# Conv attention: query projection around the output product, shared normalisation; second attention: small products in 128x32 tiles

## The chip, the cores and the metric

The kernel runs on one core of a Trainium2 chip. The metric is the device time of one execution in microseconds (us). The core has TensorE (products, and loads of the stationary operand), VectorE, ScalarE, GpSimd and SyncE (here a queue of DMA issues). Each works through its own instructions in order and waits on semaphores for the others.

## What is computed

Four images of 256 channels x 32 x 32 (1024 tokens of 256) go through three blocks. Cut to what matters:

```python
# block 1, attention by 1x1 convolutions, IC = 128
k, v, q = conv(x, wk, bk), conv(x, wv, bv), conv(x, wq, bq)           # (b, IC, n)
attn = softmax(einsum('bcn,bcm->bnm', v, q), axis=2)
o = bn2(conv(bn1(conv(einsum('bcn,bnm->bcm', k, attn), wwg)), wout))
x = relu(o + x)
# block 2, on tokens: 8 heads of 32
t = tokens(x)
q, k, v = split(layernorm(t) @ w_qkv)
t = t + softmax(q @ k.T * 256 ** -0.5) @ v @ w_out + b_out
# block 3: layer norm, router (top 2 of 8 experts), expert MLPs 256 -> 1024 -> 256 with gelu
t = t + moe(layernorm(t))
```

## The kernel before

One program is written out by hand for each engine; semaphores, each with a name, tie them together. Three phases follow each other.

**Conv phase**, `tokens(b)` for the images b = 0 to 3, in each engine's block. TensorE makes eight score blocks (`scores`), ScalarE their exponentials, TensorE weighs the keys with them (`weigh`, bank PP[3]). VectorE scales the result to `y1` in two halves. TensorE multiplies `woT` with `y1` (the output product, semaphore `cv_made`), VectorE adds the image (`cv_kept`), ScalarE applies Relu (`x1_kept`). TensorE turns the result into tokens in three groups (`turned_tokens`, line 1153: group 0 in PP[1], 1 in PP[3], 2 in PP[2]); ScalarE copies each group (lines 863 and 864, `tk_kept_a`, in the order 1, 0, 2; a copy of group 0 or 2 waits for VectorE's statistics of that group, `bst_kept`). ScalarE takes the root of the variances, VectorE normalises eight blocks of tokens to `ln` (line 1690), TensorE turns `ln` into `lnT` (line 1172, banks PP[0] and PP[1]), and ScalarE and VectorE copy it as high and low halves. Then come the query, key and value products of block 2.

Between these, for the next image b + 1, TensorE makes the first projections of block 1: `project_q` in two halves over the input channels (PP[0]), `project_v` (PP[1], which waits for the second token copy, `tk_kept_a`), `project_k` (PP[2], which waits for the third). ScalarE keeps the high halves (`keep_q`, `keep_v`), VectorE the low ones (`q_low_half`, `v_low_half`), and `keep_k`. ScalarE and GpSimd also split the expert weights into high and low halves in this phase (`split_weights(b, i)`, eight per image, with loads queued on GpSimd).

**Second attention**, `attend(b)`, 32 steps per image. A step makes four chunks of scores (`score_chunk`, line 1334, four 32-column tiles with 97 rows), the row maxima of a later group (`max_group`, line 1253, 32-row tiles; two VectorE reductions, line 1740, must leave its banks first), the weighing and the sums of an earlier step (`weigh_heads`, line 1306, and `sum_heads`, lines 1316 and 1321: 128 rows, four 32-column tiles). ScalarE makes the exponentials, GpSimd adds pairs of them. In every fourth step `max_row` turns the eight maxima of 128 queries into a row (line 1262). For b >= 1 the steps 2, 3, 4, 6, 7, 8, 10 and 11 also project 128 tokens of the image before (`tail_project`, whose products are recorded at line 1022, 128x264); VectorE adds them to the residual. The last image's eight projections stand in the last four steps, after the last two weighings, and the last two in the first expert tile.

**Experts**, 40 tiles of tokens in f16 products at full width, and the output.

Of the kernel before, what the change touches and what calls it, by code (L numbers as in the profile page):

```python
# [8 lines left out]
ALU = mybir.AluOpType  # L9
# [3 lines left out]
P = 128  # L13
B, C, N = 4, 256, 1024
CC = C // P
# [25 lines left out]


LOAD_GROUP = 16 * 7
LOAD_MAX = 16 * 2
# [70 lines left out]
def hybrid_block(nc, x, wk, bk, wv, bv, wq, bq, wwg, bn1_g, bn1_b, bn1_m, bn1_v, wout, bout,  # L115
# [20 lines left out]
    with ctx:  # L136
# [185 lines left out]
        def ring(last):  # L322
            return 2 if last else 3

        def qk_bank(u, last):
            return PP[(2, 3, 2, 0)[u]] if last else PP[(u + 2) % 4]
# [33 lines left out]
        for name in ("ld_qv ld_vec ld_first wqv_kept q_low v_low ld_w ld_x0 ld_x1 ld_y0 ld_y1 bst_kept ld_we we_kept mh_made pool_const pe_prep dve_prep act_prep "  # L360
                     "q_made v_made k_made q_kept v_kept k_kept sc_made max_kept exp_kept ks_kept "
                     "av_made y1_kept cv_made cv_kept x1_kept tk_made tk_kept_a stat_kept "
                     "sd_kept ln_kept lnT_made lnT_kept_a lnT_kept_v qk_made qhi_kept qlo_kept vt_made "
                     "vt_kept_a vt_kept_v res0_kept st_res0 st_v st_q0 st_q1 "
# [447 lines left out]
        def _(act):  # L812
# [29 lines left out]
            def tokens(b, last):  # L842
# [9 lines left out]
                for c in range(CC):  # L852
                    act.wait_ge(s("cv_kept"), b * 2 + (c + 1))
                    act.activation(XB[b][:, c], XB[b][:, c], ACT.Relu, bias=vec[:, BE2 + c:BE2 + c + 1])\
                       .then_inc(s("x1_kept"), 1)
                act.wait_ge(s("st_v"), FREE + b * 16)
                for g in (1, 0, 2):
# [10 lines left out]
                if not last:  # L868
                    keep_q(b + 1)
                    keep_v(b + 1)  # L870
                if last:
                    act.wait_ge(s("wT_made"), 1)
                    act.activation(woTf, PP[3][:, 0:HALF].rearrange("p (c i n) -> p c i n", c=CC, i=CC), ACT.Copy)\
                       .then_inc(s("wT_kept"), 1)
                else:
                    split_weights(b, 5)
                for c in range(CC):
                    act.wait_ge(s("lnT_made"), b * 2 + (c + 1))
                    act.activation(lnT[:, c, 0], PP[c][:, :], ACT.Copy).then_inc(s("lnT_kept_a"), 1)
                if last:  # L880
                    act.wait_ge(s("wp_made"), 1)
                    act.activation(wp_early[:, :, :], PP[3][:, HALF:HALF + CC * E].rearrange("p (c e) -> p c e", c=CC),
                                   ACT.Copy).then_inc(s("we_kept"), 1)
                    split_weights(b, 5)
                for u in range(4):
                    act.wait_ge(s("qk_made"), b * 4 + (u + 1))
                    if u >= 2:
                        act.wait_ge(s(f"st_q{u % 2}"), FREE + b * 64 + 32)
                    act.activation(qs[:, u % 2, 0], qk_bank(u, last)[:, :], ACT.Copy,
                                   scale=(C ** -0.5 if u < 2 else 1.0) / WSCALE).then_inc(s("qhi_kept"), 1)  # L890
                    if u < 2:
                        split_weights(b, 6 + u)
                act.wait_ge(s("vt_made"), b * 2 + 1)
                act.wait_ge(s("st_res0"), FREE + b * 16 + 16)
# [123 lines left out]
        def _(pe):  # L1018
# [22 lines left out]
            def project_q(n, c):  # L1041
                if c == 0 or not n:
                    pe.wait_ge(s(f"ld_{'xy'[n % 2]}{c}"), n // 2 * 16 + 16)
                if n and not c:
                    pe.wait_ge(s("cv_kept"), 2 * n - 1)
                    pe.wait_ge(s(f"ld_{'xy'[n % 2]}1"), n // 2 * 16 + 16)
                mm = project_half(n, PP[0], wqT, c)
                if c == CC - 1:
                    mm.then_inc(s("q_made"), 1)
# [47 lines left out]
            def tokens(b, last):  # L1097
# [35 lines left out]
                for i in range(NT):  # L1133
                    if i + ring(last) < NT:
                        scores(i + ring(last))
                    if last:
                        early_max(i)
                    weigh(i)
                for c in range(CC):
                    for h in range(2):  # L1140
                        pe.wait_ge(s("y1_kept"), b * 2 + (h + 1))
                        product(PP[c][:, h * HALF:(h + 1) * HALF], [(woT[:, c], y1[:, h * HALF:(h + 1) * HALF])],
                                "cv_made" if h else None)
                if not last:
                    project_q(b + 1, 0)
                for c in range(CC):
# [10 lines left out]
                if not last:  # L1157
                    project_q(b + 1, 1)
                    project_v(b + 1)
                    project_k(b + 1)  # L1160
                    pe.wait_ge(s("q_low"), b + 2)
                    pe.wait_ge(s("v_low"), b + 2)
                else:
# [4 lines left out]
                    router_turned()  # L1168
                for c in range(CC):
                    for t in range(NT):  # L1170
                        pe.wait_ge(s("ln_kept"), b * NT + (t + 1)) if c == 0 else None
                        mm = pe.transpose(PP[c][:, t * P:(t + 1) * P], ln[:, t, c * P:(c + 1) * P], identf[:, :])
                    mm.then_inc(s("lnT_made"), 1)
# [84 lines left out]
            def max_row(b, u, before):  # L1258

                bank = next_slot(b, before)  # L1260
                pe.wait_ge(s("nm_kept"), b * UNITS + (u + 1))
                pe.transpose(bank[0:2 * GH, 0:P], mx[:, :], identf[:, :]).then_inc(s("c_made"), 1)


            def tail_project(t, b, before, n):
# [5 lines left out]
                if n == 1 and t == 0:  # L1271
                    pe.wait_ge(s("ld_wo"), 16)
                    pe.wait_ge(s("wp_kept"), 1)
                tok_at = slice(t * P, (t + 1) * P)
                product(bank[:, 0:WIDE], [(OS[:, k, tok_at], wo_sb[:, k]) for k in range(CC)], "c_made")

# [237 lines left out]
        def _(dve):  # L1514
# [106 lines left out]
            def tokens(b, last):  # L1621
# [37 lines left out]
                for c in range(CC):  # L1659
                    dve.wait_ge(s("cv_made"), b * 2 + (c + 1))  # L1660
                    dve.scalar_tensor_tensor(out=XB[b][:, c], in0=PP[c][:, :], scalar=vec[:, S2 + c:S2 + c + 1],
                                             in1=XB[b][:, c], op0=ALU.mult, op1=ALU.add).then_inc(s("cv_kept"), 1)
                for g in (0, 2, 1):
                    made, of = turned_tokens(g)
# [22 lines left out]
                if b == 0:  # L1687
                    dve.wait_ge(s("st_zero"), 32)
                for t in range(NT):
                    dve.tensor_scalar(ln[:, t], tok[:, t], mv[:, t, 0:1], small[:, 3, t:t + 1],  # L1690
                                      ALU.subtract, ALU.mult).then_inc(s("ln_kept"), 1)
                dve.tensor_tensor(lgp[:, 0], lgp[:, 0], lgp[:, 1], ALU.add)
                dve.drain()
                dve.tensor_tensor(lg0[:, b], lgp[:, 0], per_expert(lb0[:, :], NT), ALU.add)
                if not last:
                    q_low_half(b + 1)
                    v_low_half(b + 1)
                    keep_k(b + 1)
                for c in range(CC):
                    dve.wait_ge(s("lnT_kept_a"), b * 2 + (c + 1))  # L1700
                    dve.tensor_tensor(lnT[:, c, 1], PP[c][:, :], lnT[:, c, 0], ALU.subtract)\
                       .then_inc(s("lnT_kept_v"), 1)
                dve.wait_ge(s("ln_kept"), b * NT + NT)
                dve.tensor_tensor(tok, tok, bob.unsqueeze(1).broadcast_to((P, NT, C)), ALU.add)\
# [597 lines left out]
```

## Time and profile before

| | |
|---|---|
| median of three runs | 1163.66 us (1159.1 to 1166.8) |
| the profiled execution | 1163.12 us, of which its span 1161.3 |
| TensorE busy | 1087.0 us, 94% of the span |
| VectorE, ScalarE, GpSimd busy | 816.4, 629.6, 594.3 us |
| conv phase | to about 289 us |
| second attention | about 289 to 726 us |

In the profile PE is TensorE's products, PEld its loads of weights, DVE VectorE, ACT ScalarE, POOL GpSimd, SP SyncE; L1022 is line 1022 of the kernel. One f32 product of 512 columns stands there as two records. A chain of waits is followed back from the last instruction: at each step to what released it.

### The profile page before, as it was taken

How to read it: one execution, taken by the hardware profiler on the slowest of the kernel's cores; microseconds unless marked ns; L12 is line 12 of the kernel's file. 1: busy time of each engine (PE TensorE's matmuls, PEld its weight loads, DVE VectorE, ACT ScalarE, POOL GpSimd, SP SyncE). 2: the span in 40 equal slices, each digit the busy share in tenths (PEclk: the TensorE clock that was granted, in tenths of full speed). 3: DMA queues.
4: the chain of work that ended last, by engine and by line, in shares of the span. 5: the costliest groups of instructions: out<-in, count | busy, mean ns of one | idle time of the engine just before them, and what ended most of it. 6: DMA issues, size and time to landing. Idle time of an engine off the chain costs nothing.

```text
span 1161.3 us, 34638 instructions
## 1 busy us (share of the span) xinstructions
PE 1087.0 (94%) x13440; PEld 737.8 (64%) x13440; DVE 816.4 (70%) x1489; ACT 629.6 (54%) x1144; POOL 594.3 (51%) x510
## 2 busy tenths in 40 slices
PE   7999998979899998999999989899999999999996
PEld 4464555435455555555555545688898998999884
DVE  4666666666788889788888982777565566565773
ACT  3566675645677667766775665453233333333332
POOL 3425241324588763876487456177554554453530
PEclk9999999998899999999999999999999999999997
DMA  5245851724323231533253213824332332332328
GB/s 177 91 161 202 329 173 60 236 73 154 93 63 94 75 87 35 122 85 103 70 119 93 62 46 101 309 39 92 57 47 47 57 47 48 56 44 41 47 39 294
DMA packets 98908, 121.00 MB, mean 104 GB/s; under 512 B 29024, under 2 KB 76064, under 8 KB 98112
## 3 DMA queue, kind: packets, MB, share of 16 engines
q1 hardware_dynamic: 75280, 70.40, 20.8%
q0 software_dynamic: 20400, 42.08, 15.8%
q10 hardware_dynamic: 3072, 6.30, 1.5%
q8 instruction: 113, 1.85, 0.7%
q14 instruction: 43, 0.35, 0.1%
HBM read 73.10 MB, written 45.47 MB: 102 GB/s over the span
## 4 chain that ended last, share of the span: by engine, by line
PE 70%; DVE 16%; issue 5%; DMA 3%; ACT 2%; DVEq 2%; POOL 1%; SPq 0%; ACTq 0%; POOLq 0%
PE PP L1022 23%; PE PP L1449 13%; DVE mxp L1740 9%; PE PP L1334 7%; PE PP L1306 6%; PE PP L1193 4%; PE PP L1121 4%; PE PP L1253 3%; PE PP L1038 3%; PE PP L1316 2%; PE PP L1321 2%; PE PP L1153 1%; PE PP L1408 1%; DMA res_d<-WORK,lb 1%; DVEq L2019 1%
## 5 line engine op out<-in xcount | busy, mean ns | idle before, releaser
L954 ACT ACTIVATE WB<-PP 128x512 f32<-128x512 f32 x512 | 265.3, 605 | 111.9 <-PE PP L1334 110.7
L1740 DVE TENSOR_REDUCE mxp<-PP 128x2 f32<-128x1024 f32 x242 | 287.0, 1219 | 51.3 <-PE PP L1253 50.7
L992 ACT ACTIVATE WORK<-PP,b1c 128x256 f32<-128x256 f32 (+1 forms) x320 | 139.2, 450 | 234.7 <-PE PP L1022 193.2
L698 POOL TENSOR_TENSOR WB<-WB 128x1024 f32<-128x1024 f32 x81 | 191.7, 2368 | 82.2 <-PE PP L1321 49.6
L781 POOL DMA_INDIRECT res_d<-WORK,lb x70 | 117.1, 1673 | 153.6 <-DVE WORK L2037 136.5
L1449 PE MATMUL PP<-WB,WORK 128*128 x1704 | 193.0, 273 | 0.0
L1022 PE MATMUL PP<-WORK,WB 128*128 128x256 f16 (+1 forms) x1552 | 175.8, 273 | 2.4 <-DVE WORK L2006 1.7
L1449 PEld LDWEIGHTS PP<-WB,WORK 128*128 128x128 f16 x1704 | 164.8, 98 | 19.2 <-issue 0.2
L1022 PE MATMUL PP<-WORK 128*128 128x128 f16 (+6 forms) x1086 | 162.7, 301 | 10.9 <-DVE WORK L1657 3.6
L1022 PEld LDWEIGHTS PP<-WORK,WB 128*128 (+1 forms) x1552 | 152.5, 102 | 21.6 <-issue 4.5
L1334 PE MATMUL PP<-WORK 97*32 97x256 f16 x4096 | 160.0, 276 | 5.0 <-ACT WB L954 4.5
L665 POOL TENSOR_TENSOR WB<-WORK,WB 128x1024 f16<-128x1024 f32 x32 | 68.9, 2152 | 167.7 <-ACT WORK L840 167.6
L1022 PEld LDWEIGHTS PP<-WORK 128*128 128x128 f16 (+1 forms) x1086 | 100.9, 118 | 73.8 <-issue 19.2
L1334 PEld LDWEIGHTS PP<-WORK 97*32 97x32 f16 x4096 | 91.7, 96 | 68.1 <-ACT WB L954 36.1
L1306 PE MATMUL PP<-WB,WORK 128*32 128x256 f32 x2048 | 134.8, 383 | 0.0
L2020 DVE TENSOR_TENSOR WORK<-WORK 128x512 f16<-128x512 f32 (+1 forms) x160 | 101.6, 635 | 13.0 <-issue 1.3
L771 POOL DMA_INDIRECT WORK<-rows_d,lb x70 | 71.8, 1026 | 38.9 <-issue 33.1
L2031 DVE SCALAR_TENSOR_TENSOR WORK<-PP,WORK 128x512 f32<-128x512 f32 (+1 forms) x40 | 25.2, 631 | 92.4 <-PE PP L1449 79.6
L741 POOL DMA_INDIRECT list_d<-meta,idx x64 | 63.1, 985 | 52.6 <-issue 15.0
L2018 DVE CAST WORK<-WORK 128x512 f16<-128x512 f32 (+1 forms) x160 | 64.5, 403 | 22.0 <-ACT WORK L992 17.8
L1306 PEld LDWEIGHTS PP<-WB,WORK 128*32 128x32 f32 x2048 | 60.4, 111 | 26.5 <-issue 1.6
L1253 PE MATMUL PP<-WB 32*128 32x512 f16 x484 | 48.0, 386 | 18.1 <-DVE mxp L1740 12.4
(318 smaller groups left out, 1197.3 us busy)
## 6 DMA issues: line engine op xcount, KB each, us to landing
WORK<-in_L_ffn_W_dram POOLq DMA_DIRECT2D x32, 512.0 KB, 4.1
res_d<-WORK SPq DMA_DIRECT2D x8, 1024.0 KB, 4.5
late_d<-WB POOLq DMA_DIRECT2D x1, 6144.0 KB, 19.1
WB<-late_d ACTq DMA_DIRECT2D x3, 2048.0 KB, 12.9
v_d<-WORK SPq DMA_DIRECT2D x4, 1024.0 KB, 5.7
WORK<-q_hi_d SPq DMA_DIRECT2D x16, 256.0 KB, 4.0
WORK<-v_d SPq DMA_DIRECT2D x8, 512.0 KB, 5.5
WORK<-k_hi_d SPq DMA_DIRECT2D x16, 256.0 KB, 4.4
```

What stands on the lines that cost most here:

```text
L698: pool.tensor_tensor(PS[n % 2], PR[n % 3][:, 0], PR[n % 3][:, 1], ALU.add).then_inc(s("pair_kept"), 1)
L771: pool.indirect_dma_start(xs[t % 2][:, a].rearrange("p s c -> p (s c)"), None, rows_d[0:(B if t >= EARLY else B - 1) * N, :], bass.Indirec ...
L781: pool.indirect_dma_start(res1_d[:, :], bass.IndirectOffsetOnAxis(ap=lb[:, t % LISTS, a, 1:2], axis=0), ysb[u][:, a], None, compute_op=ALU ...
L954: act.activation(PR[n % 3][:, c // 2, c % 2 * 2:c % 2 * 2 + 2], SCORES[m % 3] .rearrange("p (h n) -> p h n", h=2), ACT.Exp).then_inc(s("e_ ...
L992: act.activation(hid[:, k, 0:width], hidden_bank(k)[:, 0:width], ACT.Gelu, bias=b1c[:, bass.ds(e, 1), k], scale=1.0 / WSCALE)\
L1022: mm = pe.matmul(dst, lhsT, rhs, start=(n == 0), stop=(n == len(pairs) - 1))
L1253: mm = pe.matmul(PP[2 + h // 2][:, h % 2 * HALF:(h % 2 + 1) * HALF], QM[rows_at, g, at:at + P], KM[rows_at, g, k * HALF:(k + 1) * HALF], s ...
L1306: pe.matmul(WEIGHED[h * D:(h + 1) * D, 0:QN], VV[par][:, 2 * s4 + i, h * D:(h + 1) * D], PR[n % 3][:, i, h], start=(s4 + i == 0), stop=(s4 ...
L1334: mm = pe.matmul(SCORES[m % 3][r * D:(r + 1) * D, i * QN:(i + 1) * QN], KP[g][0:QK_ROWS + 1, h, keys], QP[0:QK_ROWS + 1, g, h, q:q + QN], ...
L1449: mm = pe.matmul(PP[2][:, u * HALF + a * C:u * HALF + (a + 1) * C], lhsT, rhs, start=(n == 0), stop=(n == len(pairs) - 1))
L1740: dve.tensor_reduce(mxp[:, n // 4 % 2, i, h:h + 2, k], PP[2 + h // 2][:, :].rearrange("p (h n) -> p h n", h=2), X_AXIS, ALU.max).then_inc( ...
L2020: dve.tensor_tensor(hs[u][:, 1, k, 0:width], hid[:, k, 0:width], hs[u][:, 0, k, 0:width], ALU.subtract).then_inc(s("hs_kept"), 1)
```

## The change

TensorE: the first half of the next image's query projection moves ahead of the output product, the second half from behind the token turning to between the two. For images 0 to 2 the output product goes to PP[2] and PP[1] in place of PP[0] and PP[1]. ScalarE keeps the queries' high half right after Relu, and VectorE the low half right after adding the image; the values' low half comes ahead of the router's sums, and only the second half of the transposes of `ln` waits for it. The normalisation is shared: VectorE five blocks, ScalarE three, with a small VectorE instruction for ScalarE's bias. `split_weights(b, 5)` moves behind the transposed copies. In the last image a small Exp is put ahead of the value copies. In the second attention the row of maxima becomes a plain product with the identity, and a projection is made as eight products of 32 tokens (two for each group of 32 rows) in place of two of 128.

```diff
+LN_SPLIT = 5
+        def conv_bank(c, last):
+            return PP[c] if last else PP[2 - c]
...
 ScalarE, tokens(b, last)
                     act.activation(XB[b][:, c], XB[b][:, c], ACT.Relu, bias=vec[:, BE2 + c:BE2 + c + 1])\
                        .then_inc(s("x1_kept"), 1)
+                if not last:
+                    keep_q(b + 1)
...
                 act.activation(small[:, 2], small[:, 1], ACT.Sqrt).then_inc(s("sd_kept"), 1)
                 if not last:
-                    keep_q(b + 1)
                     keep_v(b + 1)
+                act.wait_ge(s("rm_kept"), b + 1)
+                for t in range(LN_SPLIT, NT):
+                    act.activation(ln[:, t], tok[:, t], ACT.Identity, bias=small[:, 4, t:t + 1],
+                                   scale=small[:, 3, t:t + 1]).then_inc(s("ln_kept_a"), 1)
...
-                else:
-                    split_weights(b, 5)
                 for c in range(CC):
                     act.wait_ge(s("lnT_made"), b * 2 + (c + 1))
                     act.activation(lnT[:, c, 0], PP[c][:, :], ACT.Copy).then_inc(s("lnT_kept_a"), 1)
+                if not last:
+                    split_weights(b, 5)
...
+                if last:
+                    act.activation(rs[:, 5], rsum[:, :], ACT.Exp, scale=0.0)
                 act.wait_ge(s("vt_made"), b * 2 + 1)
...
 TensorE, project_q and tokens(b, last)
-                if c == 0 or not n:
-                    pe.wait_ge(s(f"ld_{'xy'[n % 2]}{c}"), n // 2 * 16 + 16)
-                if n and not c:
-                    pe.wait_ge(s("cv_kept"), 2 * n - 1)
-                    pe.wait_ge(s(f"ld_{'xy'[n % 2]}1"), n // 2 * 16 + 16)
+                pe.wait_ge(s(f"ld_{'xy'[n % 2]}{c}"), n // 2 * 16 + 16)
...
+                if not last:
+                    project_q(b + 1, 0)
                 for c in range(CC):
                     for h in range(2):
                         pe.wait_ge(s("y1_kept"), b * 2 + (h + 1))
-                        product(PP[c][:, h * HALF:(h + 1) * HALF], [(woT[:, c], y1[:, h * HALF:(h + 1) * HALF])],
-                                "cv_made" if h else None)
+                        product(conv_bank(c, last)[:, h * HALF:(h + 1) * HALF],
+                                [(woT[:, c], y1[:, h * HALF:(h + 1) * HALF])], "cv_made" if h else None)
                 if not last:
-                    project_q(b + 1, 0)
+                    project_q(b + 1, 1)
...
                 if not last:
-                    project_q(b + 1, 1)
                     project_v(b + 1)
                     project_k(b + 1)
                     pe.wait_ge(s("q_low"), b + 2)
-                    pe.wait_ge(s("v_low"), b + 2)
...
                 for c in range(CC):
+                    if c and not last:
+                        pe.wait_ge(s("v_low"), b + 2)
                     for t in range(NT):
-                        pe.wait_ge(s("ln_kept"), b * NT + (t + 1)) if c == 0 else None
+                        if c == 0 and t < LN_SPLIT:
+                            pe.wait_ge(s("ln_kept"), b * LN_SPLIT + (t + 1))
+                        elif c == 0:
+                            pe.wait_ge(s("ln_kept_a"), b * (NT - LN_SPLIT) + (t - LN_SPLIT + 1))
...
 TensorE, second attention
-                pe.transpose(bank[0:2 * GH, 0:P], mx[:, :], identf[:, :]).then_inc(s("c_made"), 1)
+                pe.matmul(bank[0:2 * GH, 0:P], mx[:, :], identf[:, :], start=True, stop=True).then_inc(s("c_made"), 1)
...
-                tok_at = slice(t * P, (t + 1) * P)
-                product(bank[:, 0:WIDE], [(OS[:, k, tok_at], wo_sb[:, k]) for k in range(CC)], "c_made")
+                for k in range(CC):
+                    for r in range(P // D):
+                        mm = pe.matmul(bank[r * D:(r + 1) * D, 0:WIDE], OS[:, k, t * P + r * D:t * P + (r + 1) * D],
+                                       wo_sb[:, k], start=(k == 0), stop=(k == CC - 1), skip_group_check=True)
+                mm.then_inc(s("c_made"), 1)
...
 VectorE, tokens(b, last)
-                    dve.scalar_tensor_tensor(out=XB[b][:, c], in0=PP[c][:, :], scalar=vec[:, S2 + c:S2 + c + 1],
+                    dve.scalar_tensor_tensor(out=XB[b][:, c], in0=conv_bank(c, last)[:, :], scalar=vec[:, S2 + c:S2 + c + 1],
                                              in1=XB[b][:, c], op0=ALU.mult, op1=ALU.add).then_inc(s("cv_kept"), 1)
+                if not last:
+                    q_low_half(b + 1)
...
-                for t in range(NT):
+                dve.scalar_tensor_tensor(out=small[:, 4], in0=mv[:, :, 0], scalar=-1.0, in1=small[:, 3],
+                                         op0=ALU.mult, op1=ALU.mult).then_inc(s("rm_kept"), 1)
+                for t in range(LN_SPLIT):
                     dve.tensor_scalar(ln[:, t], tok[:, t], mv[:, t, 0:1], small[:, 3, t:t + 1],
                                       ALU.subtract, ALU.mult).then_inc(s("ln_kept"), 1)
+                if not last:
+                    v_low_half(b + 1)
...
                 if not last:
-                    q_low_half(b + 1)
-                    v_low_half(b + 1)
                     keep_k(b + 1)
```

## Rows read from the trace of the kernel before

**Rows 1.** Stretches: us; busy PE, PEld, DVE, ACT, POOL; PEclk, DMA share, GB/s

```profile
112.50:135.20 22.70, 19.80 (x105) 13.63 (x106) 15.46 (x36) 12.14 (x16) 4.01 (x4) 1.00 0.93 383
...
394.80:431.00 36.20, 36.06 (x619) 19.87 (x610) 30.67 (x51) 20.51 (x41) 25.50 (x14) 1.00 0.33 79
431.00:461.30 30.30, 27.15 (x602) 15.74 (x598) 28.28 (x60) 22.44 (x46) 11.15 (x22) 1.00 0.07 17
```

**Rows 2.** Chain of waits, conv image 1: start us, us, what

```profile
112.49 0.82 DVE WORK L1657
113.36 3.70 PE PP L1022 x8
117.06 1.72 PE PP L1038 x4
118.77 3.71 PE PP L1153 x32
122.48 5.15 PE PP L1038 x12
127.63 3.57 PE PP L1022 x32
131.20 0.89 issue
```

**Rows 3.** Timeline, same stretch: start us, us, engine line, out<-in, [idle before <-releaser]

```profile
118.41 1.15 ACT L854 ACTIVATE WB<-WB,vec 128x1024 f32<-128x1024 f32 x1 [0.57 <-DVE WB L1661]
...
122.68 0.60 ACT L863 ACTIVATE WORK<-PP 128x512 f32<-128x512 f32 x1
...
123.16 0.22 ACT L864 ACTIVATE lgp<-PP 128x32 f32<-128x32 f32 x1
...
123.61 0.19 PEld L1038 LDWEIGHTS PP<-WORK 128*128 128x128 f32 x1 [0.24 <-ACT lgp L864]
...
125.98 1.10 ACT L826 ACTIVATE WORK<-PP,vec 128x1024 f16<-128x1024 f32 x1
...
129.52 1.28 DVE L1532 SCALAR_TENSOR_TENSOR WORK<-PP,vec,WORK 128x1024 f16<-128x1024 f32 x1
...
130.71 1.27 DVE L1537 SCALAR_TENSOR_TENSOR WORK<-PP,vec,WORK 128x1024 f16<-128x1024 f32 x1
...
146.71 2.07 ACT L889 ACTIVATE WORK<-PP 128x1024 f16<-128x1024 f32 x2 [3.01 <-DMA q_lo_d<-WORK]
```

**Rows 4.** Timeline, normalisation: conv image 3, and ScalarE's in the second attention

```profile
262.35 2.68 DVE L1690 TENSOR_SCALAR WORK<-WORK,mv,small 128x256 f32<-128x256 f32 x8 [0.18 <-issue]
...
262.81 4.36 PE L1172 MATMUL PP<-identf,WORK 128*128 128x128 f32 x16 [0.45 <-DVE WORK L1690]
...
444.78 0.62 ACT L923 ACTIVATE WB<-WORK,small 128x256 f32<-128x256 f32 x1
```

**Rows 5.** Timeline, start of the second attention

```profile
290.24 1.28 ACT L954 ACT_TABLE_LOAD   x1
...
290.76 2.36 DVE L1740 TENSOR_REDUCE mxp<-PP 128x2 f32<-128x1024 f32 x2 [1.67 <-PE PP L1253]
...
293.98 0.40 PE L1253 MATMUL PP<-WB 32*128 32x512 f16 x4
```

**Rows 6.** Chain of waits, second attention, image 1: two projecting steps, a plain one

```profile
416.84 0.86 PE PP L1306 x16
...
418.14 1.09 PE PP L1022 x4
419.22 0.77 PE PP L1334 x24
...
422.02 0.20 PE PP L1262
...
467.16 0.66 PE PP L1334 x22
```

**Rows 7.** Timeline of weight loads, second attention, image 1

```profile
416.56 0.66 PEld L1306 LDWEIGHTS PP<-WB,WORK 128*32 128x32 f32 x16
```

More of the change, by code:

```diff
@@ L362, in hybrid_block @@
                      "av_made y1_kept cv_made cv_kept x1_kept tk_made tk_kept_a stat_kept "
-                     "sd_kept ln_kept lnT_made lnT_kept_a lnT_kept_v qk_made qhi_kept qlo_kept vt_made "
+                     "sd_kept rm_kept ln_kept ln_kept_a lnT_made lnT_kept_a lnT_kept_v qk_made qhi_kept qlo_kept vt_made "
                      "vt_kept_a vt_kept_v res0_kept st_res0 st_v st_q0 st_q1 "
@@ L1702, in tokens @@
                        .then_inc(s("lnT_kept_v"), 1)
-                dve.wait_ge(s("ln_kept"), b * NT + NT)
+                dve.wait_ge(s("ln_kept"), (b + 1) * LN_SPLIT)
+                dve.wait_ge(s("ln_kept_a"), (b + 1) * (NT - LN_SPLIT))
                 dve.tensor_tensor(tok, tok, bob.unsqueeze(1).broadcast_to((P, NT, C)), ALU.add)\
```

## The prediction

> **What bounds the kernel now.** I read the times by stage first [rows 1], then the chain of waits through one conv batch and through the second attention [rows 2, 6], and last the timelines around the places that the diff touches [rows 3 to 5, 7]. In [rows 1] the reader is to see three kinds of stretch. Between two conv batches (112.5 to 135.2 us) TensorE is busy 19.80 of 22.70 us, so some 2.9 us of idle time per batch are there to be won. In the steps of the second attention that also project the last batch's output (394.8 to 431.0) TensorE is busy 36.06 of 36.20: there only shorter TensorE work helps. In the steps after them (431.0 to 461.3) VectorE is busy 28.28 of 30.30: there shorter TensorE work gives nothing.
>
> **The conv part, batches 0 to 2.** Old order on the path [rows 2]: VectorE makes y1 (0.82, TensorE waits 0.87, to 113.36), output product (3.70), first half of the next query projection (1.72), token turning (3.71), second half and value projection (5.15), key projection (3.57), 0.89 idle, transposes from 132.09. The idle 0.89 is the wait for `v_low`: its instruction runs from 130.71 for 1.27 us [rows 3].
>
> New: the first half runs while y1 is made, so TensorE goes from 112.49 without a pause: 1.72, then the product without its inner gap (8 pieces of 1.72 / 4 = 0.43, 3.44), then 1.72 of the second half, then 3.71 of turning. The turning ends at 112.49 + 1.72 + 3.44 + 1.72 + 3.71 = 123.08, 0.60 later than the 122.48 of before, but with all of the query projection done. The wait for y1 is gone (0.87 and 0.26 inside the product) and so is the wait for `v_low`, since `v_low` now comes ahead of `keep_k` and is asked for only by the second half of the transposes. Removed: 2.02 us.
>
> What is late next is the value projection. It writes the bank that the second copy of the turned tokens (group 0) must have left, and before, the second half of the query projection stood between turning and value projection and covered that: already there a weight load sat behind this copy, at 123.61, 0.23 after the copy's end at 123.16 + 0.22 = 123.38 [rows 3]. Nothing covers it now. ScalarE's copies follow the turning, so they come 0.60 later, and group 0 is left at 123.98; plus 0.23 plus one load of 0.19 gives a first value product at 124.40, where TensorE could have begun at 123.08: 1.3 us of new idle time. Then 3.44 of value and 3.57 of key projection end at 131.41, where the transposes can start at once: 132.09 - 131.41 = **0.68 us per batch, 2.0 us for three**.
>
> This holds if the inserted `keep_q` and `q_low` don't delay the copy further. The second Relu ends at 118.41 + 1.15 + 0.60 = 120.16, `keep_q` takes 1.10, `q_low` 1.28 [rows 3]: VectorE is free at about 122.5, 0.8 us before the copy at 122.68 + 0.60, for the two statistics that the copy waits for. It is tight, so I bound the conv part: 0 where the copy comes 0.7 later still, 132.09 - (123.08 + 3.44 + 3.57) = 2.0 per batch, 6.0 in all, where no wait is left. I take 2.0, since the rows of both sides of the wait are there.
>
> Normalisation is no limit any more: VectorE's five, after one small instruction, and ScalarE's three of about 0.6 [rows 4] are done before 131.4, as the copies end 0.6 later and eight on VectorE alone took 2.68. I cost them at nothing; without the cover of the key projection the share that ScalarE takes would be worth 3 x 0.33. `split_weights(b, 5)`, moved behind the transposed copies, delays GpSimd's low half and the next weight load, and ScalarE may stand before split 7. What is queued behind it there, the third high half, waited 3.01 us for a store anyway [rows 3]: cost nothing, up to 0.5 per batch if the load is slow, inside the lower bound.
>
> **The last conv batch.** Eight normalisations took 2.68 us and pace the first transposes, whose 16 took 4.36 [rows 4]. Five plus the small instruction are some 1.9. Between 0 and 0.75 I take 0.5, because the remaining transposes stay. The Exp put ahead draws the table load of 1.28 us (290.24) into a time when ScalarE waits for the value product. The next group of row maxima then can't start before VectorE has ended its reductions, 290.76 + 2.36 = 293.12, where it started at 293.98 [rows 5]: 0.9, bounds 0 and 1.28.
>
> **The second attention: the projection in 128x32 tiles.** In the chain one projection of 128 tokens takes 1.09 us, and the 24 score products after it 0.77, where they take 0.66 behind 32-column work [rows 6]. Its bare streaming is what `weigh_heads` shows: 16 pieces (8 products of 256 columns, f32, 32-wide) in 0.86. The new projection has the same 8 products with 264 columns: 0.86 x 264 / 256 = 0.89. So it costs 0.89 + 0.66 in place of 1.09 + 0.77: **0.31 saved**, all of it the entry to and exit from the full-width form, and nothing in arithmetic. VectorE can follow: in that stretch it is busy 30.67 of 36.20 us [rows 1], and eight projections shorten it by 2.5, to 33.7. 24 projections within steps: 7.4 us. Bounds: 0.2 each where only the entry is saved (4.8), 0.31 for all.
>
> Of the eight projections at the end, five are followed by 32-column work (5 x 0.31) and the sixth saves 0.2. The last two stand in the first expert tile, among full-width products: they now pay entry and exit, 0.3 together. 1.4 in all, between 0.7 and 1.8.
>
> The rule that speaks against: the Trainium skill (TensorE: Matmul & The Clock Gate, section Part 3, packing small matmuls) says a weight load overlaps running products only where its row group differs, and here all four tiles use all rows. By it the loads of the new projection would be laid bare, and the sum would turn from a gain of 13.2 into a loss, the rival of the bare loads below. This trace disagrees: the 16 loads of `weigh_heads`, 0.66 in all [rows 7], lie inside its 0.86.
>
> **The row of maxima as a plain product.** 31 of them. Before, 0.20 plus 0.11 for the switch [rows 6]. A 32-column product of 256 columns lasts 0.43 in its tile (two rounds in 0.86), so 128 columns 0.21, or 0.11 if neighbours overlap: 0.1 to 0.2 saved, and only where TensorE is the bound and VectorE's copy of the row isn't, some 7 of 31: 1.0 us, between 0 and 2.
>
> **Sum.** 2.0 + 0.5 + 0.9 + 7.4 + 1.4 + 1.0 = 13.2 us. The profiled execution took 1163.12 us, close to the median 1163.66, so 1149.9: **1150 us**. The low bounds give 5.5 us (1157.6), the high ones 19 us (1144).
>
> **Rivals.**
> *The conv gain is all lost* in the wait for group 0's copy or in the delayed weight split: 13.2 - 2.0 = 11.2, 1152. For it speaks that the slack of 0.8 us is small. 0.16.
> *The value projection doesn't wait*, or less: up to 4 us more, 1146. Against it, that weight load right behind the copy at 123.61. 0.10.
> *The tiles pack worse than in `weigh_heads`.* There each tile streams its own operand; here the four share one. If what is gained per projection falls from 0.31 to about 0.1, 30 projections give 3 in place of 8.8: 1156. 0.10. The Trainium skill, same section, has three column tiles at 2.38 times one; by that ratio four would do the work of 3.2, a projection would take about 1.1, and the gain nearly vanishes as in this rival; the 0.86 in this trace shows no such loss.
> *The loads of the tiles are laid bare.* 0.66 more for each of 32 projections is 21 us: 1171. Against it, [rows 7] within [rows 6]. 0.03.
> *Slower: the four tiles run one after the other.* Place: every projection. Price: 8 x 0.44 = 3.5 us in place of 0.89, 2.6 more than forecast, 32 times: 84 - 13 = 71 us slower, about 1234. It decides from where a projection takes 13.2 / 32 = 0.41 more than the forecast 0.89. Against it: the same 32-wide f32 products run four abreast in [rows 6]. 0.03.
> *My forecast*, own range 1146 to 1154: 0.58.
>
> **How the numbers follow.** A measurement of this kernel tells about 1% from no change, here the line at 1152.0. My case lies mostly under it (0.46 of 0.58), the second rival wholly (0.10), the first in part (0.05): faster 0.61. Slower 0.03, the rest 0.36. The range for 8 in 10 runs from 1144 to 1158: all bounds of the sum, the first three rivals, and not the last two.
>
> **What would show it.** In the profile after: no idle time before the output product; a new wait of about 1.3 us before the value projection, released by ScalarE's group copy; transposes right behind the key projection; 0.89 for a projection and 0.66 for the score products after it; the table load ahead of the value copies. The steps with a projection should take 3.57 us where they took 3.88. What would make me wrong: a wait for the row of maxima's stores, whose slack in steps shrinks by some 0.6 us, or VectorE taking over as bound in the projection steps, where 3.0 us in 33.7 are left to it.

## The result, and the profile after

The changed kernel takes 1166.55 us (median of 11 runs, 1161.91 to 1171.02) where the kernel before takes 1162.79 us beside it (11 runs): a ratio of 1.0035, 95% interval 1.0020 to 1.0051. It is no faster, and a little slower; the forecast was 1150 us, and 1166.55 lies outside its range. The profiled execution took 1168.45 us, with a span of 1166.5.

Where the time went is seen by cutting both profiled executions at fixed marks (starts in the timelines: `y1` of each image, the first score chunk, the 25th projection, the two projections in the first expert tile). The last two columns are versions of the experiments below: e1 has the whole change but for the place of split 5, e11 also takes back the last three narrow projections.

| stage, us | before | after | e1 | e11 |
|---|---|---|---|---|
| start to first `y1` | 49.65 | 49.93 | 49.68 | 49.49 |
| image 0 | 62.84 | 63.69 | 61.74 | 61.74 |
| image 1 | 62.77 | 67.01 | 61.74 | 61.74 |
| image 2 | 73.31 | 75.27 | 70.63 | 72.31 |
| last image, to the first score chunk | 40.52 | 41.91 | 40.13 | 40.20 |
| to the 25th projection | 418.31 | 414.04 | 411.35 | 410.28 |
| to the two in the expert tile | 24.07 | 24.75 | 26.25 | 22.59 |
| experts | 429.83 | 429.90 | 429.38 | 430.05 |
| span | 1161.3 | 1166.5 | 1150.9 | 1148.4 |

To the 25th projection the second attention gains 4.3 us. The three conv batches (images 0 to 2), where 2.0 us were to be won, lose 7.1. Image 2 can only be compared to within some 2 us: it holds a stretch of TensorE at half clock in the kernel before and in e11, and none in e1, which has the same code there as e11. The chain of waits of the changed kernel through conv image 1 shows both what was won there and what took it (start us, us, what):

```profile
113.58 1.72 PE PP L1049 x4
115.29 3.43 PE PP L1033 x8
118.73 1.72 PE PP L1049 x4
...
125.10 3.70 PE PP L1049 x8
128.80 3.57 PE PP L1033 x32
132.37 0.89 PE PP L1184 x8
...
133.28 1.94 ACT WORK L886 x2
135.22 0.94 ACT WB L843
136.16 0.95 ACT WORK L844
...
137.20 3.70 POOL WB L669
...
141.18 8.00 DMA WORK<-in_L_ffn_W_dram
...
149.20 0.34 ACT WB L843
...
151.11 1.01 ACT WORK L898
...
152.15 0.95 DVE WORK L1730
```

Its first rows answer to [rows 2]: the wait of 0.87 before the product is gone, and the transposes (132.37) follow the key projection without a pause. From 135.22 on the chain leaves TensorE: split 5 on ScalarE (L843, L844), GpSimd's low half (3.70), the weight load that this releases (8.00), split 7, and only then the third high half (L898, 151.11). ScalarE, VectorE and TensorE stood still for it. ScalarE in the timeline:

```profile
149.20 1.06 ACT L843 ACTIVATE WB<-WORK 128x1024 f16<-128x1024 f32 x1 [7.30 <-DMA WORK<-in_L_ffn_W_dram]
```

TensorE still had its value products to make (48, until 151.04). It waited 3.60 us for the low halves that follow the third and fourth high half, and made the next 24 products at half clock (PEclk 0.50, the lower of its two levels, 1.2 of 2.4 GHz; columns as in [rows 1]). In e1 the 48 and the 24 stand in one row, without a wait. Timeline and windows of the changed kernel, then the timeline of e1:

```profile
154.65 7.03 PE L1033 MATMUL PP<-WORK 128*128 128x512 f16 x24 [3.60 <-DVE WORK L1730]
```

```profile
157.00:159.00 2.00, 2.00 (x6) 0.70 (x5) 0.66 (x2) 1.39 (x3) 0.00 (x0) 0.50 0.96 342
```

```profile
143.44 10.72 PE L1033 MATMUL PP<-WORK 128*128 128x256 f16 x72
```

In images 0 and 2 the same wait of TensorE is 1.80 and 2.06 us. The clock stayed up behind the first, and fell behind the second.

In the kernel before, split 7 (L839) waits for nothing: the load was issued at 133.18, by its DMA row it lands 4.8 us later, and ScalarE comes to it at 141.70:

```profile
133.18 0.78 POOL L648 DMA_DIRECT2D WORK<-in_L_ffn_W_dram  x1 [0.30 <-POOL WB L665]
```

```profile
141.70 1.06 ACT L839 ACTIVATE WB<-WORK 128x1024 f16<-128x1024 f32 x1
```

What waited there was the third high half, 3.01 us for a store [rows 3]. In images 0 and 2 of that kernel the same wait is only 1.01 and 1.05 us.

### The profile page after: what moved, and what is told of

Read it like the earlier page. It is cut to its first block, busy times and chain, and to the rows that moved or that the text cites. A ratio compares the mean times of both kernels' runs of the same rounds, so it can differ in the third digit from the quotient of the medians.

```text
span 1166.5 us, 35474 instructions
## 1 busy us (share of the span) xinstructions
PE 1084.8 (93%) x13855; PEld 745.1 (64%) x13855; DVE 811.0 (70%) x1481; ACT 635.5 (54%) x1157; POOL 599.8 (51%) x510
## 4 chain that ended last, share of the span: by engine, by line
PE 62%; DVE 17%; DMA 7%; issue 6%; ACT 3%; DVEq 2%; POOL 1%; SPq 1%; POOLq 0%; ACTq 0%
PE PP L1033 19%; PE PP L1464 13%; DVE mxp L1760 10%; PE PP L1349 5%; PE PP L1321 5%; PE PP L1265 4%; PE PP L1128 3%; PE PP L1049 3%; DMA res_d<-WORK,lb 3%; PE PP L1288 2%; PE PP L1331 2%; DMA WORK<-in_L_ffn_W_dram 2%; PE PP L1336 1%; PE PP L1423 1%; PE PP L1205 1%
## 5 line engine op out<-in xcount | busy, mean ns | idle before, releaser
L1349 PE MATMUL PP<-WORK 97*32 97x256 f16 x4096 | 166.1, 276 | 4.7 <-ACT WB L965 2.3
L669 POOL TENSOR_TENSOR WB<-WORK,WB 128x1024 f16<-128x1024 f32 x32 | 73.5, 2297 | 170.6 <-ACT WORK L844 170.5
L1033 PE MATMUL PP<-WORK 128*128 128x128 f16 (+3 forms) x958 | 129.1, 291 | 14.6 <-DVE WORK L1730 7.5
L1349 PEld LDWEIGHTS PP<-WORK 97*32 97x32 f16 x4096 | 102.3, 96 | 60.4 <-ACT WB L965 33.7
L1033 PEld LDWEIGHTS PP<-WORK 128*128 128x128 f16 (+1 forms) x958 | 80.2, 110 | 64.5 <-issue 32.0
```

The source lines that it names most:

```text
L669: pool.tensor_tensor(lo, stage[:, i % 2, :], hi, ALU.subtract).then_inc(s("split_lo"), 1)
L1033: mm = pe.matmul(dst, lhsT, rhs, start=(n == 0), stop=(n == len(pairs) - 1))
L1349: mm = pe.matmul(SCORES[m % 3][r * D:(r + 1) * D, i * QN:(i + 1) * QN], KP[g][0:QK_ROWS + 1, h, keys], QP[0:QK_ROWS + 1, g, h, q:q + QN], ...
```

## Experiments

| version | median us | ratio to before | 95% interval |
|---|---|---|---|
| the change | 1166.55 | 1.0035 | 1.0020 to 1.0051 |
| e1: without the moved split | 1154.52 | 0.9928 | 0.9900 to 0.9956 |
| e2: the moved split alone | 1171.95 | 1.0078 | 1.0056 to 1.0099 |
| e3: second attention alone | 1160.85 | 0.9984 | 0.9966 to 1.0003 |
| e4: conv part alone, split not moved | 1158.97 | 0.9971 | 0.9957 to 0.9984 |
| e5: split 7 later | 1161.72 | 0.9996 | 0.9976 to 1.0015 |
| e7: e4 and the row's product | 1160.63 | 0.9991 | 0.9972 to 1.0011 |
| e8: e1, query projection in quarters | 1154.85 | 0.9951 | 0.9933 to 0.9969 |
| e9: e1, row transposed | 1154.86 | 0.9939 | 0.9916 to 0.9962 |
| e10: e1, normalisation not shared, no early Exp | 1159.11 | 0.9983 | 0.9968 to 0.9998 |
| e11: e1, last three projections at full width | 1152.32 | 0.9927 | 0.9907 to 0.9946 |

e6 and e12 were executed once each (1190.91 and 1160.14 us), so they have no interval.

### Is it the moved split? (e1, e2)

e1 takes it back in the changed kernel, e2 puts it alone into the kernel before.

```diff
+                else:
+                    split_weights(b, 5)
                 for c in range(CC):
                     act.wait_ge(s("lnT_made"), b * 2 + (c + 1))
                     act.activation(lnT[:, c, 0], PP[c][:, :], ACT.Copy).then_inc(s("lnT_kept_a"), 1)
-                if not last:
-                    split_weights(b, 5)
```

> The changed kernel, with one edit undone: ScalarE's weight split 5 stands again ahead of the copies of the transposed tokens. Theory A (the moved split starts GpSimd's low half and the next weight load late, ScalarE then stands 5.5 to 7.3 us before split 7 and TensorE behind it): the wait before split 7 goes away in all three conv batches, the three batches take about 62, 62 and 72 us in place of 63.7, 67.0 and 75.3, and the kernel takes about 1156 to 1158 us. Theory B (the reordered query projection, its new wait before the value projection, or the shared normalisation cost what was lost): the batches stay within 1 us of what they are in the changed kernel, 1164 to 1167 us.

> The kernel before, with one edit of the change alone: split 5 behind the copies of the transposed tokens. Theory A: the same wait before split 7 arises, some 2 to 5 us per batch, 1170 to 1174 us. Theory B: within 2 us of the kernel before, 1161 to 1165 us.

Theory A held in both, though e1 came out 1.5 us below the times that I gave. Without the move the change gains 0.7%, and the batches take 61.74, 61.74 and 70.63 us. The move alone costs 0.8%, and the same wait stands in its trace, 7.58 us long:

```profile
151.57 1.06 ACT L839 ACTIVATE WB<-WORK 128x1024 f16<-128x1024 f32 x1 [7.58 <-DMA WORK<-in_L_ffn_W_dram]
```

The move buys nothing either: from the start of `y1` to the first product of the attention's projections e1 takes 133.07 - 111.42 = 21.65 us and the changed kernel 135.27 - 113.62 = 21.65, since ScalarE is done with split 5 in e1 (130.07 + 1.05) just as the transposed tokens come to be copied (131.08).

### Why 7 us and not 2? (e5, e6)

Split 5 comes 6.4 us later than before (135.10 against 128.68), 5.3 us later counted from the start of `y1` in each kernel (113.62 and 112.49). With the kernel before's 2.1 us for the low half and 4.8 us for this load, the load would be down at 137.20 + 2.1 + 0.3 + 4.8 = 144.4, 2.5 us after ScalarE wants it (141.90). But the low half took 3.70 and the load 8.0. e6 takes away what ran beside them: VectorE's addition to the tokens (L1724), and with it their store, go behind the second low half.

```diff
-                dve.tensor_tensor(tok, tok, bob..., ALU.add).then_inc(s("res0_kept"), 1)
                 for u in range(4):
                     ...
+                    if u == 1:
+                        dve.tensor_tensor(tok, tok, bob..., ALU.add).then_inc(s("res0_kept"), 1)
```

> The changed kernel with VectorE's addition of the output bias to the tokens moved behind the second low half, and with it the store of these tokens. If GpSimd's low half of split 5 takes 3.70 in place of 2.13 us because that addition runs beside it, it takes 2.1 here; if the next weight load takes 8.0 in place of 4 us because the stores run beside it, it lands in 4 to 5 us here. Rival: both keep their long times (3.7 and 6 to 8 us), so the cause lies elsewhere. The time itself may go either way, since the stores behind the addition come later.

Timelines, first the changed kernel, then e6:

```profile
136.61 2.28 DVE L1724 TENSOR_TENSOR WORK<-WORK 128x2048 f32<-128x2048 f32 x1
137.20 3.69 POOL L669 TENSOR_TENSOR WB<-WORK,WB 128x1024 f16<-128x1024 f32 x1 [21.97 <-ACT WORK L844]
```

```profile
144.56 2.12 POOL L669 TENSOR_TENSOR WB<-WORK,WB 128x1024 f16<-128x1024 f32 x1 [22.17 <-ACT WORK L844]
146.97 0.78 POOL L652 DMA_DIRECT2D WORK<-in_L_ffn_W_dram  x1 [0.30 <-POOL WB L669]
...
151.22 1.06 ACT L843 ACTIVATE WB<-WORK 128x1024 f16<-128x1024 f32 x1 [1.95 <-DMA WORK<-in_L_ffn_W_dram]
...
159.25 1.02 ACT L898 ACTIVATE WORK<-PP 128x1024 f16<-128x1024 f32 x1 [6.03 <-DMA q_lo_d<-WORK]
```

Both guesses hold: 2.12 in place of 3.69, and the load lands in 4.2 us. ScalarE waits 1.95, the part that the late start alone makes. So ScalarE's 7.3 us are 2.5 (the late start) + 1.6 (GpSimd beside VectorE) + 3.2 (the load beside the stores). GpSimd's excess of 1.57 us is about its overlap with the addition (137.20 to 138.89, 1.69 us). The Trainium skill (SBUF — State Buffer, section Who interferes with whom) says that a VectorE instruction with two inputs in SBUF contends with a GpSimd instruction that reads SBUF, and calls the port pair that these two engines share an exclusive lock; the trace agrees with that. e6 is no way out: the stores now come too late, and the third high half waits 6.03 us for them.

e5 asks the other way whether the load would cost nothing if the high halves did not stand behind it: split 5 stays late, split 7 goes behind the value copy.

```diff
-                    if u < 2:
+                    if u < 1 or (last and u < 2):
                         split_weights(b, 6 + u)
                 ...                                   # value copy
+                if not last:
+                    split_weights(b, 7)
```

> The changed kernel with split 5 where it has it (behind the transposed copies), but with split 7 moved from behind the second high half to behind the value copy, so that the third and fourth high halves no longer stand behind the wait for the late weight load. Theory A1 (the loss is the high halves queued behind that wait, the late load costs nothing by itself): the third high half waits about 3 us for the store of the low half, as in the kernel before, the batches take 62 to 63 and 71 to 73 us, about 1156 to 1159 us. Rival A2 (the late load itself holds up the next image's splits and loads, wherever the wait stands): the loss turns up at the next batch's exponentials, 1162 to 1167 us.

Neither A1 nor A2 as I had put them. Only some 5 of 12 us come back: the three waits of TensorE shrink to 0.51, 2.35 and 0.39 us. ScalarE no longer waits for the load, but the high half waits as long for its store:

```profile
147.74 1.02 ACT L898 ACTIVATE WORK<-PP 128x1024 f16<-128x1024 f32 x1 [7.27 <-DMA q_lo_d<-WORK]
```

The transfers slow each other. The DMA rows of the short stretch in which the load is issued (last column: us from issue to landing) are, for the changed kernel and for e1, where it runs ahead of the stores:

```profile
WORK<-in_L_ffn_W_dram POOLq DMA_DIRECT2D x1, 512.0 KB, 8.0
...
q_lo_d<-WORK SPq DMA_DIRECT2D x1, 256.0 KB, 8.7
```

```profile
WORK<-in_L_ffn_W_dram POOLq DMA_DIRECT2D x1, 512.0 KB, 4.6
...
q_lo_d<-WORK SPq DMA_DIRECT2D x1, 256.0 KB, 5.8
```

So the price of the move is a transfer pushed out of an open place into the stretch of the stores, and whichever of the two ScalarE waits for, it waits about 7 us in this image and 5.5 to 6.0 in the other two.

### What is the second attention's part worth? (e3, e12, e4, e7, e9, e11)

e3 and e12 are the same kernel: the kernel before with `tail_project` in four tiles and `max_row` as a product.

> The kernel before, with the second attention's part of the change alone: the projection in 128x32 tiles and the row of maxima as a plain product. If the 0.24 us per step that the changed kernel shows holds (24 steps, then 1.2 at the end and 0.7 for the rows), 1155 us; if the fall of TensorE's clock seen between 570 and 574 us belongs to the new forms, 1157 to 1158 us; if nothing of it reaches the end, 1163 us. The three conv batches take what they take in the kernel before, 62.8, 62.8 and 73.3 us.

> The kernel before with the second attention's part of the change alone, a second profile of the same kernel (its time was 1160.9, where 24 steps at 0.24 us gave 1155). Theory: its steps are as short as in the first profile (about 106.4 us for eight projections with a quarter of the maxima, and 91.5 us), and what is missing to 1155 us lies in stretches where TensorE's clock is granted at half. Rival: the steps themselves are longer, as in the kernel before (108.6 and 94.2 us).

e3's median moved by a sixth of a per cent, with an interval that includes no change. Yet the steps are short in both profiles: from the first projection of one image to that of the next it takes 106.4 us where no stretch at half clock falls in (in e3; 108.6 in the kernel before), and for the last image 91.5 (93.1 in e4, below). The chain of the changed kernel shows the step, and what is missing to the 0.31 that I forecast:

```profile
403.77 0.89 PE PP L1288 x16
404.66 0.66 PE PP L1349 x24
405.31 0.06 issue
405.38 0.40 PE PP L1265 x4
405.77 0.33 PE PP L1349 x8
```

0.89 and 0.66 came true to the hundredth; 0.06 of a new wait before the maxima leaves 0.25. The rest of the missing time goes with TensorE's clock. Three times in the second attention TensorE waits 1.72 us for VectorE's row maxima, in both kernels. Behind such a wait the clock can fall to half, here in e12 (windows: us; busy PE, PEld, DVE, ACT, POOL; PEclk, DMA share, GB/s):

```profile
456.00:458.00 2.00, 0.77 (x28) 0.47 (x20) 2.00 (x3) 1.55 (x3) 1.28 (x2) 1.00 0.00 0
458.00:460.00 2.00, 1.51 (x24) 0.77 (x28) 1.97 (x6) 0.75 (x3) 0.00 (x0) 0.84 0.04 2
460.00:462.00 2.00, 2.00 (x32) 1.13 (x28) 1.47 (x3) 0.36 (x1) 0.00 (x0) 0.50 0.13 42
```

Over all profiles of this study, those with the narrow projection show such a fall behind 11 of 30 of these waits (10 profiles), those with the wide one behind 1 of 12 (4 profiles). Counts this small can still be chance. The mean clocks of the timed runs say the same of e3 (0.983, against 0.987 for the kernel before; on 1160 us that is some 4.5 us, an estimate), and not of e1 (0.987). That the tiles make a fall likelier is what these numbers speak for, and it is not shown; why they would, no run shows.

e4 has the conv part and not the second attention's; e7 adds the row's product to it, e9 the tiles.

> The kernel before, with the convolution's part of the change alone, and without the moved split: query projection around the output product, shared normalisation, the Exp ahead of the value copies. Theory A: 1.0 us gained in each of the three conv batches and 0.5 to 1 at the change to the attention, about 1159 us. Theory B: 1163 us or more, since the reorder itself loses.

> The changed kernel with split 5 back ahead of the copies and with the projection at full width again; the plain product for the row of maxima stays. Against the version with all parts (1154.5) it shows what the 128x32 projection is worth, against the version without the second attention's part (1159.0) what the row of maxima is worth. Theory: projection 24 x 0.24 + 1.2 = 7, row 0.7, so 1158 us. Rival from the low gain of the second attention's part on its own: projection 1 to 2 us, 1155 to 1156 us.

> The changed kernel with split 5 back ahead of the copies and the row of maxima as a transpose again; the projection stays in 128x32 tiles. Against the version with all parts (1154.5) it shows what the plain product for the row is worth. My prediction had 1.0 us for it, so 1155.5 us here. Rival from the two versions without the tiles (1159.0 with the transpose, 1160.6 with the product): the product is worth nothing or costs up to 1.7 us, so 1153 to 1154.5 us here.

e4 confirms 1.0 per batch: 61.74 us in the first two images, and in the third 70.63, without the stretch at half clock (some 1.7 us) of the kernel before. e7 came out above both of the times that I gave, e9 between its two. To the 25th projection e4 takes 416.82 us and e7 416.85: the row's product is worth nothing there. In time e7 is 0.2% behind e4 and e1 0.1% ahead of e9, with intervals that overlap: no difference can be measured. The tiles are worth 0.3% (e4 to e9) to 0.6% (e7 to e1).

e11 puts the last three projections back to full width.

```diff
             def final_project(c):
                 slots[0] = c
-                tail_project(c, B - 1, FINAL_SLOTS, B)
+                tail_project(c, B - 1, FINAL_SLOTS, B, wide=c >= 5)
```

> The changed kernel with split 5 back ahead of the copies, and the last three of the 32 projections (the one right before the experts, the two in the first expert tile) at full width again. If the longer unexplained wait before the first expert transposes (2.1 us in place of 1.35 where the projection is narrow) is TensorE's own issuing of 32 loads and products in place of 8, it falls to about 1.35 here and the two projections among full-width products lose their entry and exit: 0.5 to 1.0 us faster, 1153.5 to 1154 us. Rival: that wait is for something that arrives at a fixed time; then it stays at about 2 us and the time at 1154.5.

Its theory held for the wait. TensorE's rows at the change to the experts, e1 first, then e11:

```profile
712.48 1.06 PE L1288 MATMUL PP<-WORK 128*32 128x264 f32 x16
715.69 1.01 PE L1423 MATMUL PP<-ident,WORK 128*128 128x128 f16 x8 [2.15 <-issue]
717.58 4.02 PE L1033 MATMUL PP<-WORK,WB 128*128 128x256 f16 x18 [0.88 <-DVE WORK L2026]
```

```profile
712.19 1.16 PE L1033 MATMUL PP<-WORK 128*128 128x264 f32 x4
714.71 0.61 PE L1427 MATMUL PP<-ident,WORK 128*128 128x128 f16 x8 [1.36 <-issue]
716.19 2.16 PE L1033 MATMUL PP<-WORK,WB 128*128 128x256 f16 x18 [0.88 <-DVE WORK L2030]
```

The wait is shorter by 0.8, and what follows runs at full clock: 2.16 us for 18 products that took 4.02. In the nine profiles with a narrow projection before the experts the wait is 2.1 to 2.2, and the clock falls behind it in seven; in the five with a wide one it is 1.3 to 1.4, and the clock never falls. In ratio e11 and e1 are equal (0.9927, 0.9928), so by time the 2.2 us between their medians are not shown; both are faster than the kernel before and than the change.

### The rest of the conv part (e10, e8)

e10 is e1 with `LN_SPLIT = 8` and without the Exp ahead of the value copies.

> The changed kernel with split 5 back ahead of the copies, VectorE alone normalising all eight blocks, and no Exp ahead of the value copies. My prediction: nothing in the first three batches as long as the key projection covers the eight normalisations, 0.5 us in the last batch, 0.9 us at the first row maxima of the attention, so 1155.9 us where all parts take 1154.5. Rival: without the share of ScalarE the transposes wait in the first three batches too (eight normalisations of 0.34 after the statistics end at about 128.9, then the low half of the values): 62.5 us per batch in place of 61.74, 1157 to 1158 us.

The rival held, by another way than it said. The batches take 62.64, 62.51 and 72.98 us, 0.8 to 0.9 more for the first two (the third holds a stretch at half clock, e1's doesn't). The transposes don't wait; VectorE's queue is late behind them:

```profile
130.04 1.27 DVE L1550 SCALAR_TENSOR_TENSOR WORK<-PP,vec,WORK 128x1024 f16<-128x1024 f32 x1
131.14 2.31 POOL L669 TENSOR_TENSOR WB<-WORK,WB 128x1024 f16<-128x1024 f32 x1 [16.79 <-ACT WORK L844]
131.24 0.21 DVE L1711 TENSOR_TENSOR lgp<-lgp 128x64 f32<-128x64 f32 x1
131.53 2.00 DVE L1713 TENSOR_TENSOR lg<-lgp,lb 128x64 f32<-128x64 f32 x1
133.45 1.21 DVE L1624 TENSOR_TENSOR WORK<-PP,WORK 128x1024 f32<-128x1024 f32 x1
...
134.81 1.89 PE L1203 MATMUL PP<-WORK 128*128 128x512 f16 x8 [1.48 <-DVE WORK L1624]
...
136.98 8.81 PE L1203 MATMUL PP<-WORK 128*128 128x512 f16 x40 [0.29 <-DVE WORK L1718]
```

TensorE waits 1.48 us (1.16 in e1) for `keep_k` (L1624), which stands behind the normalisations, `v_low` and an addition that now takes 2.00 in place of 0.22 beside GpSimd's low half, and 0.29 more for the low half of the transposed tokens (L1718) behind that. From the first chunk to the first projection e10 takes 106.84 us, e1 105.98: 0.9, as forecast for the early table load. Over all profiles this stretch takes 106.3 to 106.8 us without the early load (five) and 104.7 to 106.0 with it (nine), so the sign is clear and the size is not.

e8 goes after the new wait of 0.95 us before the value projection: e1, with the last quarter of the query projection behind the turning, and the token copies and kept halves reordered for it.

```diff
-                    project_q(b + 1, 1)
+                    project_q(b + 1, 1, (0,))
                 ...                                   # token turning
+                    project_q(b + 1, 1, (1,))
                     project_v(b + 1)
```

> The changed kernel with split 5 back ahead of the copies, and against the new wait before the value projection: the last of the four pieces of the query projection (0.86 us) stands behind the token turning, ScalarE copies the tokens of group 0 first, and the kept halves of the queries go behind the statistics again. If the wait of 0.95 us before the value projection is what is left in the conv batches, they gain 0.6 more each, about 1152.5 us; if the later query halves hold up the transposes instead, 1154 to 1156 us.

Inconclusive. The batches take 60.85, 62.33 and 69.73 us, the first and third 0.9 less than e1's and the second 0.6 more; in time it is not ahead of e1.

## Why the prediction was wrong

**The step that failed is the cost of the moved split: "cost nothing, up to 0.5 per batch if the load is slow".** Against e1 it cost 2.0, 5.3 and 4.6 us in the three batches, 12 us in all (1166.55 against 1154.52); 7.5 of these are the three waits of TensorE (1.80, 3.60, 2.06), and most of the rest goes with its clock at half, behind the second and third wait and once more in image 2. The path was named rightly (GpSimd's low half, the next load, ScalarE before split 7, the third high half behind it). What failed are the times put into it. I let the low half, the load and the store that the third high half waits for take at the new place what they had taken at the old one: 2.1, 4.8 and 6.0 us in image 1 of the kernel before. At the new place they took 3.7, 8.0 and 8.7, because VectorE's addition and the stores run just there; I had not looked at what runs there. Load and store landed only at 149.2 and 149.5, and TensorE stood behind them.

The lateness alone need not have cost anything. An estimate from rows of image 1: with the old times the load is down at 144.4, split 7 (1.9 us) done at 146.3, and the store down at 140.76 + 6.0 = 146.8; TensorE, busy until 151.04 and 3.54 us behind the third high half (151.11 to 154.65), would have had it in time until 147.5. e6 bears out the first half of this: with a load of 4.2 us split 7 is done at 153.2, 5.2 us before TensorE's value products end at 158.4. No run has the late split with all of its transfers at their old times. And the cover was thinner than I took it for: the 3.01 us [rows 3] are those of image 1, and the other two have 1.0.

**The rival "the conv gain is all lost" named the cause and priced it too low.** It ended at zero gain, so the range could not hold a loss.

**The conv part else held.** The new wait before the value projection is 0.95 (1.3 forecast), released by ScalarE's group copy as named; the gain is 1.05 per batch (0.68). The normalisation was costed at nothing for these batches on the ground that TensorE did not wait for it; it is worth 0.8, through VectorE's queue. So the reorder without that share gave only 0.2 to 0.3 (e10's first two batches against the kernel before), less than the 0.68, and that the two together passed the forecast is luck. The 0.5 of the last batch can't be read: from its `y1` to the first chunk five profiles with the same code there (e1, e4, e7, e9, e11) take 40.1 to 43.3 us.

**The second attention was right in its pieces, and too large in its sum.** Projection and chunks are 0.89 and 0.66; the step is 3.63 to 3.64, not 3.57. (The loads in [rows 7] begin 0.28 us ahead of the 0.86 of [rows 6], beside the score products, and do not lie wholly inside it; that they overlap running products stands.) To the 25th projection the profiles gain 3.7 (e4 to e9) to 5.5 us (e7 to e1) by the tiles, where 7.4 were forecast. The projections at the end, from the 25th to the two in the expert tile, win 0.5 and 0.85 us in the two profiles whose clock held there (e6, e3) and lose 0.3 to 2.2 in the seven where it fell; 1.4 were forecast. I had charged entry and exit for the last two, not the longer wait behind the eight small products in front of the experts, nor the clock behind that. The row's product, 1.0, is worth nothing measurable. The bare loads and the serial tiles did not happen, and VectorE took no more from the projecting steps than the 0.06.

**The early table load** gave the 0.9 forecast in the pair e10 and e1, between 0.3 and 2.2 over all profiles.

## What to carry to other kernels

Moving work later is costed along its own chain: what it releases, how much slack that had, and what runs at the new place on the same port and the same DMA engines. The times to use are those of the new place, also for the wait that is to hide it. A wait elsewhere on the engine hides nothing unless it ends later than the new arrival. An engine that nobody waits for now can be the one that everybody waits for once the neighbour is shortened, so the queue behind a shortened or lengthened instruction is read to its end.

## What the runs showed of the hardware

- GpSimd's 128x1024 subtraction took 3.70 us beside a VectorE addition of two SBUF operands (the changed kernel), and 2.12 without it (e6); a 128x64 addition of VectorE took 2.00 us beside GpSimd's subtraction (e10) in place of 0.22.
- The load of 512 KB for split 7 landed in 3.8 to 4.8 us ahead of the stores (the kernel before, e1, e4, e6, e7) and in 6.2 to 8.3 beside them (the change, e2, e5); the first store of a low half took 4.0 to 6.0 (the kernel before, e1, e4, e7) and then 6.9 to 9.0.
- With a projection of eight narrow products just ahead of the expert tile, the wait there that the profile calls issue took 2.1 to 2.2 us (nine profiles), with one of two wide products 1.3 to 1.4 (five). What TensorE does in it, no run shows.
- TensorE's clock fell to half behind waits of 1.7 to 2.2 us in some executions and not in others of like kernels, at about 1.7 to 3.4 us each time.
